# A two-layer decoder on one core: five of nine FP4 weight-scaling multiplies move from GpSimd to VectorE, with the scheduler's table that goes with them

## The reference, cut to what matters

```python
x = _layernorm(x + _L0_attn_ref(x, ...))             # decayed running sum, then o_w
x = _layernorm(x + _L0_xattn_ref(x, ctx, ctx, ...))  # 16 heads, rope, softmax
x = _layernorm(x + _L0_ffn_ref(x, w_gate, w_up, w_down))   # FP4 (E2M1) feed-forward
x = _layernorm(x + _L1_attn_ref(x, ...))             # linear attention and a GELU MLP
x = _layernorm(x + _L1_xattn_ref(x, ctx, ctx, ...))
x = _layernorm(x + _L1_ffn_ref(x, ...))              # mixture of 8 experts, top 2
```

```python
def fp4_quant_dequant(x):
    xb = x.reshape(shape[:-1] + (shape[-1] // 16, 16))
    scale = jnp.maximum(jnp.max(jnp.abs(xb), axis=-1, keepdims=True) / 6.0, 1e-12)
    xn = xb / scale
    idx = jnp.searchsorted(_MID, jnp.abs(xn))
    q = _GRID[idx] * jnp.sign(xn) * scale
```

## Time and profile before

| | |
|---|---|
| median of three runs | 1003.78 us (1001.34 to 1004.27) |
| the profiled execution's own time | 1003.78 us |
| its span, first to last instruction | 1001.7 us |
| PE busy | 892.8 us (89% of the span) |
| DVE busy | 614.1 us (61%) |
| ACT busy | 508.9 us (51%) |
| POOL busy | 303.7 us (30%) |
| mean granted TensorE clock | 0.966 of full speed |

### The profile page before, as it was taken

One profiled execution on the slowest core, in us unless ns is written; L12 is line 12 of the kernel. 1 busy time (PEld: TensorE's weight loads), 2 busy tenths in 40 slices (PEclk: granted clock), 3 DMA queues, 4 the chain that ended last, 5 costly groups with the idle time before them and its releaser, 6 DMA issues.

```text
span 1001.7 us, 20256 instructions
## 1 busy us (share of the span) xinstructions
PE 892.8 (89%) x7498; PEld 711.4 (71%) x7498; DVE 614.1 (61%) x1815; ACT 508.9 (51%) x1207; POOL 303.7 (30%) x485
## 2 busy tenths in 40 slices
PE   3669899999999889899899999999999999789990
PEld 2446668667787667687678778777787888679880
DVE  4998775677765778857767676777653544003203
ACT  1335446563647464454555456465545664336642
POOL 4423322222333124331222422242321233215424
PEclk9679999999999999999999999999999999899995
DMA  9999000000010000000000031131211248989954
GB/s 329 400 319 330 9 1 12 12 7 17 17 38 22 18 17 7 22 28 11 7 8 15 27 112 54 59 128 59 96 54 32 86 135 272 378 278 394 403 201 177
DMA packets 39425, 115.01 MB, mean 115 GB/s; under 512 B 5464, under 2 KB 21600, under 8 KB 38688
## 3 DMA queue, kind: packets, MB, share of 16 engines
q1 hardware_dynamic: 35584, 103.46, 29.6%
q0 software_dynamic: 3744, 10.26, 2.7%
HBM read 99.25 MB, written 37.70 MB: 137 GB/s over the span
## 4 chain that ended last, share of the span: by engine, by line
PE 57%; DVE 19%; ACT 7%; issue 6%; DMA 5%; SPq 3%; POOL 1%; ACTq 0%; DVEq 0%; POOLq 0%
PE ps L707 39%; PE ps L712 7%; PE ps L719 5%; PE ps L783 3%; DVE PT L1106 2%; DMA EW<-moe_w 2%; DVE stat L1047 2%; ACT PT L1418 2%; ACT slot_rows L1418 1%; DMA work<-xs_d 1%; PE ps L850 1%; DVE sm L1063 1%; PE ps L1008 1%; DVE PT L1071 1%; DVE stat L1048 1%
## 5 line engine op out<-in xcount | busy, mean ns | idle before, releaser
L1606 POOL TENSOR_TENSOR stat<-stat,mhalf 128x1 f32<-128x1 f32 x112 | 66.7, 596 | 308.6 <-DVE stat L1049 308.4
L707 PE MATMUL ps<-wall,slot_rows 128*128 128x256 f32 (+1 forms) x448 | 131.0, 420 | 11.0 <-ACT KB L1445 9.0
L707 PEld LDWEIGHTS ps<-wall,slot_rows 128*128 128x128 f32 x448 | 78.5, 191 | 34.4 <-issue 22.3
L712 PE MATMUL ps<-cst,PT 128*128 128x128 f32 x512 | 73.5, 280 | 15.2 <-DVE PT L1106 4.2
L1106 DVE TENSOR_REDUCE PT<-ps 128x8 f32<-128x1024 f32 x64 | 75.3, 1219 | 15.2 <-PE ps L719 15.1
L719 PE MATMUL ps<-KB 32*128 32x128 f32 (+1 forms) x2048 | 77.3, 287 | 7.6 <-DVE PT L1106 2.4
L719 PEld LDWEIGHTS ps<-KB 32*128 32x128 f32 (+1 forms) x2048 | 65.3, 190 | 25.6 <-issue 20.3
L707 PEld LDWEIGHTS ps<-slot_rows,wall 128*128 128x128 f32 x640 | 75.3, 192 | 9.0 <-issue 4.2
L707 PE MATMUL ps<-slot_rows,wall 128*128 128x128 f32 x640 | 78.9, 277 | 2.5 <-ACT PT L1500 0.9
L707 PE MATMUL ps<-wgu,slot_rows 128*128 128x352 f32 x256 | 79.5, 462 | 1.7 <-DVE PT L1106 0.9
L712 PEld LDWEIGHTS ps<-cst,PT 128*128 128x128 f32 x512 | 59.0, 143 | 30.3 <-issue 15.9
(11 more groups left out here) (228 smaller groups left out, 1858.2 us busy)
## 6 DMA issues: line engine op xcount, KB each, us to landing
EW<-moe_w SPq DMA_DIRECT2D x30, 514.0 KB, 4.9
EW<-moe_w SPq DMA_DIRECT2D x30, 512.0 KB, 5.8
PT<-moe_w SPq DMA_DIRECT2D x12, 514.0 KB, 8.0
PT<-moe_w SPq DMA_DIRECT2D x12, 512.0 KB, 9.6
wall<-wts SPq DMA_DIRECT2D x1, 4104.0 KB, 20.0
work<-xs_d SPq DMA_DIRECT2D x31, 129.0 KB, 4.1
slot_rows<-ys_d SPq DMA_DIRECT2D x8, 384.0 KB, 8.2
KB<-ys_d SPq DMA_DIRECT2D x8, 384.0 KB, 5.9
```

The source lines that it names most:

```text
L707: last = k.e.matmul(o, a, b, start=(i == 0), stop=(i == len(pairs) - 1))
L712: last = k.e.transpose(ps[:, u.at, c * P:(c + 1) * P], src[:, c * P:(c + 1) * P], ident)
L1606: return k.e.tensor_tensor(v[:, 7:8], v[:, 8:9], mhalf[:, :], ALU.pow)
```

## The change

For the even parts (i = 0, 2, 4, 6 and 8) the multiplication by the block scales moves from POOL to DVE, as a new last step after the tail; DVE waits for its own tail first (`k.after`). The odd parts stay on POOL, and the semaphore `wy_ready` now counts odd parts alone. In the planner's table the piece of an even part has 0.7 us of DVE more instead of 1.2 us of POOL.

```diff
@@ plan_weights
-        yield piece(work=[("D", 1.4, None), ("P", 1.2, ("wq", i))],
+        yield piece(work=[("D", 1.4, None), ("P", 1.2, ("wq", i)) if i % 2 else ("D", 0.7, ("wq", i))],
                     needs=[("abs", i)])
@@ new, beside dve_fp4_tail
+        def dve_fp4_scale(k, dst, n, tmp, small):
+            m = n // DH
+            return k.e.tensor_tensor(v3(dst, DH), v3(tmp[1], DH),
+                                     bc(small(1)[:, 0:m].unsqueeze(2), m, DH), ALU.mult)
@@ dve_weights
-                dve_fp4_tail(k, tmp).then_inc(wy_ready, 1)
+                if i % 2:
+                    dve_fp4_tail(k, tmp).then_inc(wy_ready, 1)
+                else:
+                    k.after(k.step(dve_fp4_tail(k, tmp)))
+                    dve_fp4_scale(k, part, width, tmp, small).then_inc(wq_even, 1)
@@ pool_weights
-                m = width // DH
-                part, y = v3(raw[f][0][:, lo:lo + width], DH), v3(wq_part(i, width)[1], DH)
-                k.wait_ge(wy_ready, i + 1)
-                k.e.tensor_tensor(part, y, bc(ws[:, i % 2, 1, 0:m].unsqueeze(2), m, DH), ALU.mult).then_inc(
-                    wq_odd if i % 2 else wq_even, 1)
+                if i % 2:
+                    m = width // DH
+                    part, y = v3(raw[f][0][:, lo:lo + width], DH), v3(wq_part(i, width)[1], DH)
+                    k.wait_ge(wy_ready, i // 2 + 1)
+                    k.e.tensor_tensor(part, y, bc(ws[:, 1, 1, 0:m].unsqueeze(2), m, DH), ALU.mult).then_inc(wq_odd, 1)
```

## The result

The changed kernel is slower. Its median is 1010.96 us (1006.34 to 1013.15) against 1004.21 us (1001.34 to 1007.78) for the kernel before, nine runs each; the ratio is 1.0061, with a 95% interval of 1.0038 to 1.0085. By the ratio that is 6.1 us where 1.8 were forecast (the ratio is estimated from all the runs; the two medians alone lie 6.75 us apart).

The account below looks back on a forecast made before the run. TensorE was taken as the limit from 150 to 850 us, DVE in the opening. Opening +1.9, seam -1.4, tables -0.6, middle 0 and end +1.9 gave +1.8 us on 1003.78: 1005.6 us, range 998.5 to 1011.

Parts of the forecast that it names:

- The opening: Weight scaling up to 78 us: new DVE steps cost 3.4 us, less savings, +1.9 us; bounds +1.0 and +3.4.
- Two savings: In the opening, DVE steps no longer held up by POOL: 0.7 us at L1064, 0.3 at part 8's L1070.
- the cover of 0.5: DVE's idle 1.21 us before part 7's tail hides 0.52 us of part 6's scaling.
- the first rival: Opening costs in full, seam gives nothing: 1008.5 us, chance 0.25; decided if the sample's L1070 starts over 3 us later.
- The seam: Around 100 us, new pieces fill half of PE's 2.81 us wait before sample 2's product: -1.4 us; bounds 0 and -4.5.
- the 2 us that were asked: Sign for the forecast: PE's wait before sample 2's product falls below 2 us in the profile after.
- ACT's tables: ScalarE needs 55 function-table loads instead of 57, taken at 0.3 us each: -0.6 us; bounds 0 and -2.6.
- The end: From 850 us, sample 15's store ahead of `EW0`'s load delays that load: +1.9 us; bounds 0 and +3.9.
- The rival that the end does not change: The store finds its rows ready, so the end costs nothing: 1003.7 us, same; chance 0.15.
- The middle: From 150 to 850 us, only PE's 30.7 us of idle time can change: 0, with 3 us each way.
- The sign that I had named: PE's idle time from 150 to 850 us changing by over 4 us would show the order made the result.
- the slower rival: Opening costs in full and the seam gives nothing: +4.7 us, 1008.5 us; chance 0.25.

Follow-up runs that it names:

- the two runs with the old order and the new work: Changed kernel's five scalings on DVE, but the order of all engines as in the kernel before, run twice: ratios 1.0041 and 1.0035 to the kernel before.
- after: The changed kernel, with scalings moved to DVE and the planner's new order, against the kernel before: ratio 1.0061, and 1.0061 when repeated.
- the new order with old work: All scalings on POOL as in the kernel before, but engines in the changed kernel's order: ratio 1.0051 to the kernel before.
- that edit: Changed kernel with five matmuls on constants put into PE's wait of 2.15 us at 367.78 us: ratio 1.0025 to the kernel before.
- the third order: Changed kernel with 0.8 us instead of 0.7 of DVE in the planner's table for an even part's scaling, giving another order: ratio 1.0058 to the kernel before.

## Why the prediction was right or wrong

**The opening, +1.9: right in kind, measured +1.1.** That is the sum of the terms below; the two runs with the old order and the new work have +1.4 and +0.8 from first to second mark. The heads and tails of after, DVE's rows by time:

```profile
22.80 0.35 DVE L1064 TENSOR_SCALAR X<-X 128x32 f32<-128x32 f32 x1
...
26.20 0.69 DVE L1071 SCALAR_TENSOR_TENSOR work<-work 128x512 f32<-128x512 f32 x1
26.92 0.69 DVE L1075 TENSOR_TENSOR EW<-work,X 128x512 f32<-128x512 f32 x1
...
28.24 0.18 DVE L1064 TENSOR_SCALAR X<-X 128x32 f32<-128x32 f32 x1
...
68.82 0.69 DVE L1070 SCALAR_TENSOR_TENSOR X<-X 128x512 f32<-128x512 f32 x1 [0.72 <-ACT X L1393]
...
74.99 0.69 DVE L1070 SCALAR_TENSOR_TENSOR work<-work 128x384 f32<-128x384 f32 x1
76.45 0.56 DVE L1075 TENSOR_TENSOR work<-work,X 128x384 f32<-128x384 f32 x1
76.93 0.42 DVE L1070 SCALAR_TENSOR_TENSOR PT<-PT 128x256 f32<-128x256 f32 x1
```

The new step takes 0.69 us, and 0.56 for the small part, as worked out. Two savings were larger. L1064 fell to 0.18 us and not to 0.36: the row of 0.36 at 22.09 that I took for the free one was itself stretched by POOL. Four times 0.36 are 1.4, not 0.7. At part 8 two of the sample's steps, L1070 and L1071, had been stretched beside POOL (0.95 and 0.56 us, now 0.42 and 0.43), 0.7 us instead of 0.3. The idle time ahead of part 7's tail shrank from 1.21 to 0.72, the cover of 0.5 as forecast. Only 0.3 us went the other way, since L1070 and L1071 of the small part are now stretched (0.69 for 0.55). In sum 3.4 - 1.4 - 0.7 - 0.5 + 0.3 = 1.1. The sample's L1070 that began at 74.48 now begins at 76.93, of which 0.7 us are this execution's later start: 1.7 later, so the first rival's test (more than 3) was not met. DVE's busy time rose by 2.2 us (forecast 2.4), POOL's fell by 5.6 (5.1).

**The seam, -1.4: right in place, measured -0.8 (the new order with old work, first to second mark).** The new order has ten more instructions done by then, some 1.5 us of PE's work, so the gain is larger than that by up to as much. The wait of 2.81 us before sample 2's product is gone, and one of 1.64 stands a piece earlier, below the 2 us that were asked. PE's row of after, and the stretch behind it:

```profile
104.32 0.66 PE L956 MATMUL ps<-cst,work 128*128 128x128 f32 x4 [1.64 <-ACT PT L1427]
```
```profile
104.00:109.00 5.00, 4.68 (x57) 4.02 (x58) 3.72 (x11) 4.78 (x12) 1.61 (x3) 1.00 0.01 2
```

**ACT's tables, -0.6: not to be seen.** There are 55 loads as read from the order, but nothing in the traces that could be put down to the two that are gone.

**The end, +1.9: wrong, about 0.** The rival that the end does not change was right here. The store stands ahead of `EW0`'s load, but it did not hold it up. The chain of waits of after, with the store's own row from SP's timeline ahead of it:

```profile
866.27 0.33 SPq L1845 DMA_DIRECT2D ys_d<-X  x1
```
```profile
866.81 0.11 SPq L1882
...
867.36 6.35 DMA EW<-moe_w
```

The store went at 866.27, and SP then still stood until ACT let it go on at 866.81. I had put the count (L990) some 2.4 us further ahead of that point; it moved by 4.1: from 11.5 us ahead (845.53 to 857.03) to 15.6 (851.20 to 866.81). PE's waits for expert weights from 850 to 900 us are

```profile
PE ps L707 <- DMA EW<-moe_w: 10.2, 6, 4.1
```

10.2 us against 9.7 in a stretch 10 us longer, and behind the third mark the two kernels take the same time (-0.1 us).

**The middle, 0: the step that failed.** "PE's work is the same, so only its 30.7 us of idle time can change" counts idle time alone. It did not change, not by 0.1 us, and still the time from second to third mark made +8.1 of the +8.1 us, through the clock, most of it behind the waits. The sign that I had named for a result made by the order, idle time changed by more than 4 us, could not have shown it; the number of instructions in the 700 us, or the 0.98 in the clock's column, could. And the rows for it were there: I had read a clock of 0.66 behind the wait of 2.81 us at the seam, and did not ask where the new order would make such waits in the middle. Where these fall can't be read from the order; that a new order of 700 us can only lose by the clock, when before has none of them at 1.2 GHz, could have been.

**In sum.** The forecast's terms without the middle, as measured, are +1.1 - 0.8 + 0 + 0 = +0.3 for its +1.8; the middle, which stood at 0 with 3 each way, makes up the rest of the 8.1 us between the two traces (6.1 by the ratio of all runs). That the median of 1010.96 lies below the range's end of 1011 is luck: that end was made of the slower rival and 3 us of scatter, not of a fallen clock. This rival came nearest in time (1008.5) with a mechanism that was not the cause.

**Shown, argued and open.** Shown: the new order alone makes the kernel slower; it does so at a lower clock and with no more idle time; and the clock stays up behind a wait that is filled. Shown by pairs of executions with the same instructions: that falls of 3.4 us cost 1.3 to 1.7 us each in the new order. Argued from the traces alone: that the falls make the whole of the order's loss, since only one of them was taken away by an edit, and that edit's ratio moved by more than its place gave. Open: why the moved work in the old order costs 3.5 to 4.1 us by the ratios when its opening is later by 0.8 to 1.4. Its runs have 69 and 73 us at the lower level against before's 65, which at 0.25 us for one makes 1 to 2 us more, and I could not find what in the order or the waits brings that about. It is also open what decides at the waits of 0.8 to 1.9 us, where the clock falls in some executions and not in others, and what brings the falls at 823 us and, in the third order, at 286 us. And why the two parts of the change, 0.51% and 0.35 to 0.41% alone, make 0.61% together was not tried; the intervals are 0.17 to 0.25 points each way.

## What to carry to other kernels

Where an order, a planner's table or a cost is touched in a kernel that TensorE bounds, compare the longest single waits of PE and the granted clock of the stretches, not only the sum of idle time: with equal idle time in fewer, longer waits the trace was 8 us of 1000 longer here. Such a wait could be filled with matmuls on constants where a PSUM bank was already claimed; at the one that was for the banks themselves no run put any. To price such a fall, compare two executions of the same kernel instruction by instruction. And when a duration is to be the undisturbed one, take it where the other engine idles: the "free" 0.36 us was twice the real 0.18.

## What the runs showed of the hardware

- The clock's falls have a part that repeats and one that does not. At the waits of 1.93, 2.25 and 2.40 us of the new order it went to 1.2 GHz in five traces of five, behind the one of 1.89 us at 222 us in three of five, and behind the one of 1.50 us at 363 us of the old order in two of six, with the same instructions on both sides. At 823 us it fell in both traces of after with no wait ahead; what did that was not tried.
- A fall of 3.4 us to 1.2 GHz moved all that stood behind it by 1.3 to 1.7 us, where two executions of the same instructions differ by it; over all executions the slope is 0.25 us of span for a microsecond.
- A VectorE operation with one input and 32 elements a partition (L1064) takes 0.18 us while GpSimd rests and 0.35 to 0.84 beside it. The Trainium skill (SBUF — State Buffer, "SBUF: two separate sides") has the lock for operations with two SBUF inputs or in a 2-port mode; the trace agrees in that L1064 ends with POOL's instruction. It has one input, and whether it ran in a 2-port mode no run shows.
- The start of a run scatters more than many an edit brings: the first mark lies between 26.8 and 30.6 us, and DVE's very first instruction took 0.8 us or 5.47.
